# Preparation and first attention merged into one pipeline, with the bf16 remainders' subtractions on VectorE

## The reference

```python
def _L0_xattn_ref(q, k, v):          # q = layernorm(x), k = v = ctx_2048
    b, d, m = q.shape                # 64, 64, 256;  h = 8 heads
    qh = q.reshape(b * h, d // h, m)
    kh = k.reshape(b * h, d // h, -1)
    vh = v.reshape(b * h, c // h, -1)
    scale = 1.0 / jnp.sqrt(d // h)
    qk = jnp.einsum('bdm,bdn->bmn', qh, kh) * scale
    sm = jax.nn.softmax(qk, axis=-1)
    ret = jnp.einsum('bmn,bcn->bcm', sm, vh)
    return ret.reshape(b, c, m)

x = x + _L0_xattn_ref(_layernorm(x, axis=-1), ctx_2048, ctx_2048)
```

## Time and profile before

| | |
|---|---|
| Three runs | 2029.39, 2031.86, 2032.33 us |
| Median | 2031.86 us |
| Profiled execution, its span | 2031.3 us |
| TensorE (PE) busy | 1408.2 us, 69% |
| VectorE (DVE) busy | 1363.5 us, 67% |
| ScalarE (ACT) busy | 1120.5 us, 55% |
| GpSimd (POOL) busy | 497.0 us, 24% |
| First score matmul of the attention | 134.1 us |
| First instruction of the stage behind the attention | 580.1 us |

### The profile page before, as it was taken

The page is one execution under the profiler, slowest core; times in us unless marked ns, Lnnn a source line. Parts: engine busy times, 40 slices in busy tenths (PEclk is TensorE's granted clock), DMA queues, the critical chain, the costliest instruction groups (busy, mean ns, idle before and its releaser), DMA issues. The chain is left out here.

```text
span 2031.3 us, 33248 instructions
## 1 busy us (share of the span) xinstructions
PE 1408.2 (69%) x11186; PEld 870.4 (43%) x11186; DVE 1363.5 (67%) x2850; ACT 1120.5 (55%) x1552; POOL 497.0 (24%) x903
## 2 busy tenths in 40 slices
PE   4429999999929894999626667379999646674111
PEld 4305555555527771555411333246565423342100
DVE  6646888888634534588867999535555468875896
ACT  4516777777712222677637888633434237875554
POOL 4411233333320004111013343200101001112663
PEclk9999999999959996999855766689999958877555
DMA  5652555555330003233110000011010120000111
GB/s 168 204 131 54 123 131 132 131 129 131 87 86 1 0 1 59 49 73 76 33 67 0 0 1 1 16 42 43 22 41 22 34 87 1 0 1 11 42 52 42
DMA packets 96387, 117.99 MB, mean 58 GB/s; under 512 B 29728, under 2 KB 82152, under 8 KB 91660
## 3 DMA queue, kind: packets, MB, share of 16 engines
q1 hardware_dynamic: 96268, 116.46, 23.0%
HBM read 80.07 MB, written 22.88 MB: 51 GB/s over the span
## 5 line engine op out<-in xcount | busy, mean ns | idle before, releaser
L610 DVE TENSOR_REDUCE ratt_nmax<-ratt_psS 128x2 f32<-128x512 f32 x512 | 318.7, 684 | 100.3 <-PE ratt_psS L502 98.7
L576 ACT ACTIVATE ratt_E<-ratt_psT 128x1024 f32<-128x1024 f32 x256 | 255.1, 1023 | 111.7 <-PE ratt_psT L524 111.6
L502 PE MATMUL ratt_psS<-ratt_K,ratt_Q 72*128 72x256 bf16 x1024 | 205.0, 285 | 42.9 <-DMA ratt_K<-context_parts 37.7
L524 PE MATMUL ratt_psT<-ratt_Q,ratt_K 75*128 75x256 bf16 x1024 | 196.8, 276 | 7.6 <-DMA ratt_Q<-ratt_rows 7.2
L502 PEld LDWEIGHTS ratt_psS<-ratt_K,ratt_Q 72*128 72x128 bf16 x1024 | 80.3, 99 | 139.5 <-issue 67.5
L537 PE MATMUL ratt_psO<-ratt_E,ratt_V 128*32 128x256 f32 x2048 | 138.8, 389 | 0.7 <-ACT ratt_E L576 0.7
L524 PEld LDWEIGHTS ratt_psT<-ratt_Q,ratt_K 75*128 75x128 bf16 x1024 | 99.9, 99 | 25.8 <-DMA ratt_Q<-ratt_rows 7.7
L3393 PE MATMUL final_psT<-final_identh,final_Z 128*128 128x128 f16 x64 | 8.3, 311 | 110.2 <-ACT final_Z L3427 110.2
L2195 PE MATMUL nffn_psH<-nffn_W,nffn_QT 128*128 128x512 bf16 x128 | 56.2, 589 | 28.8 <-ACT nffn_H L2274 19.9
L537 PEld LDWEIGHTS ratt_psO<-ratt_E,ratt_V 128*32 128x32 f32 x2048 | 53.8, 110 | 50.9 <-issue 28.1
L892 ACT COPY sffn_XS<-sffn_psG 128x512 f32<-128x512 f32 x8 | 4.7, 586 | 124.0 <-PE sffn_psG L841 124.0
(11 more groups left out here) (472 smaller groups left out, 3703.4 us busy)
## 6 DMA issues: line engine op xcount, KB each, us to landing
ratt_Q<-z_parts SPq DMA_DIRECT2D x32, 576.0 KB
ratt_K<-context_parts SPq DMA_DIRECT2D x96, 192.0 KB
gatt_V<-in_ctx_dram SPq DMA_DIRECT2D x16, 512.0 KB, 6.3
z_parts<-prep_ZS SPq DMA_DIRECT2D x48, 128.0 KB, 2.6
context_parts<-prep_CS SPq DMA_DIRECT2D x48, 128.0 KB, 2.3
head_sums<-ratt_O SPq DMA_DIRECT2D x64, 72.0 KB
all_X<-in_x_dram SPq DMA_DIRECT2D x8, 512.0 KB
prep_C<-in_ctx_dram SPq DMA_DIRECT2D x8, 512.0 KB
```

What stands on the lines that cost most here:

```text
L502: mm = nc.tensor.matmul(psS[:, RING[h], c * D:(c + 1) * D], Q9[0:R, buf, h, k % 2, c * P:(c + 1) * P], K9[0:R, buf, h, k % 2, :], start=Tr ...
L524: mm = nc.tensor.matmul(psT[:, p % 2, e, c, :], K9[0:RM, buf, h, u, c * P:(c + 1) * P], Q9[0:RM, buf, h, u, :], start=True, stop=True)
L576: nc.scalar.activation(E[:, 2 * b + p // 2, 2 * (p % 2):2 * (p % 2) + 2], psT[:, p % 2], ACT.Exp, scale=SCALE).then_inc(exped, 1)
L610: nc.vector.tensor_reduce(nmax[:, k % 2, h, :], psS[:, RING[h]].rearrange("p (c t) -> p c t", c=2), AX.X, ALU.max, negate=True).then_inc(m ...
```

## The change

The two functions become one, `first_attention`. Its slots begin at n = -12 (LEAD), and the preparation of a pair of tiles (a, 16 of them, in place of eight groups of four tiles) is spread over the slots 4a - 12 to 4a - 4, in the same per-engine programs as the attention: `at(n, r)` gives the pair whose step r falls on slot n. There is no barrier between the two, and no loop: all slots are written out. The parts of C and Z have one buffer for a pair, Z one, C two; the remainders overwrite C and Z. By step: 0 loads, 1 transpose of C (into the ring psT) and VectorE's statistics, 2 aggregates, first part and remainder of C, 3 GpSimd's root and second part of C, 4 normalisation, third part of C, product with the weights, 5 first part of Z and the sum for ST, 6 remainder and second part of Z, 7 third part of Z. A part is stored one slot later or in the same one (steps 3 to 8).

The engines of some steps differ from before: all four subtractions are VectorE's (C's were GpSimd's), the two second parts' casts are GpSimd's (were ScalarE's), the third parts are written by the subtraction itself, in bf16 (were a subtraction and a cast of ScalarE's), the normalisation is ScalarE's (was VectorE's), and ST comes from a product of GpSimd's and a reduction of VectorE's (was TensorE's). The functions of the attention's own steps stay as they are, but for the ring psT, in which the transpose of C takes a place.

```diff
@@ -74,226 +74,7 @@
-def prepare(nc, io, X, CT, ident, zq, ck, ST, wsum):
...
-def row_attention(nc, io, X, CT, ident, identb, zq, ck, o_dram, r_dram):
+def first_attention(nc, io, X, CT, ident, identb, zq, ck, o_dram, r_dram, ST, wsum):
...
+    LEAD = 12
+    WEIGHTS = 9
...
+        C = s.sb("C", [P, 2, 2, D])
+        Z = s.sb("Z", [P, 2, D])
+        CS = s.sb("CS", [P, 3, 2, D], BF16)
+        ZS = s.sb("ZS", [P, 3, 2, D], BF16)
...
+        def at(n, r):
+
+            a, left = divmod(n + LEAD - r, 4)
+            return a if left == 0 and is_pair(a) else None
+
+        job, jobs = {}, 0
+        for n in range(-LEAD, UNITS + LAG + 1):
+            for p in range(4):
+                if is_unit(n - LAG):
+                    job["shift", n - LAG, p] = jobs
+                    jobs += 1
...
+                def load_x(a):
+                    if a > 1:
+                        sp.wait_ge(x_in[a % 2], a // 2 * 16)
+                    sp.dma_start(X[:, 2 * a:2 * a + 2, :],
+                                 x_dram[2 * a:2 * a + 2].rearrange("t p d -> p t d")).then_inc(x_in[a % 2], 16)
+
+                def load_c(a):
+                    if a > 1:
+                        sp.wait_ge(c_third, a - 1)
+                    sp.dma_start(C[:, a % 2],
+                                 c_dram[2 * a:2 * a + 2].rearrange("t p d -> p t d")).then_inc(c_in[a % 2], 16)
+
+                def store_c(a, part):
+                    sp.wait_ge((c_first, c_second, c_third)[part], a + 1)
+                    sp.dma_start(ck.rearrange("r s a h u m -> s a h r (u m)")[part, a],
+                                 CS[:, part].rearrange("p u m -> p (u m)")).then_inc(c_out, 16)
+
+                def store_z(a, part):
+                    sp.wait_ge((z_first, z_second, z_third)[part], a + 1)
+                    sp.dma_start(zq.rearrange("s r a h u m -> s a h r (u m)")[part, a],
+                                 ZS[:, part].rearrange("p u m -> p (u m)")).then_inc(z_out, 16)
+
...
+                for n in range(-LEAD, UNITS + 11):
                     if is_unit(n - 1):
+                        bring_row(n - 1)
+                    if n % 2 and is_unit(n + 3):
+                        load_q((n + 3) // 2)
+                    if n % 2 == 0 and is_unit(n + 2):
+                        load_k((n + 2) // 2)
+                    c = n // 4 - 2
+                    if n % 4 == 0:
+                        if is_pair(c - 1):
+                            inverses_out(c - 1)
+                        if is_pair(c):
+                            out(c)
+                    if n % 4 == 1 and is_pair(c):
+                        sums_back(c)
+                    if n % 4 == 2 and is_pair(c - 1):
+                        back(c - 1)
+                    if at(n, 0) is not None:
+                        load_x(at(n, 0))
+                        load_c(at(n, 0))
+                    for part in range(3):
+                        if at(n, 3 + part) is not None:
+                            store_c(at(n, 3 + part), part)
+                        if at(n, 6 + part) is not None:
+                            store_z(at(n, 6 + part), part)
...
+                def root(a):
+                    pool.wait_ge(z_agg, a * 2 + 2)
+                    gp.tensor_tensor(veps[:], mv[:, :, 1], eps[:], ALU.add).then_inc(z_pool, 1)
+                    pool.wait_ge(z_pool, a * 3 + 1)
+                    if a > 0:
+                        pool.wait_ge(z_done, a * 2)
+                    gp.tensor_tensor(rstd[:], veps[:], mhalf[:], ALU.pow).then_inc(z_pool, 1)
+                    pool.wait_ge(z_pool, a * 3 + 2)
+                    gp.tensor_tensor(shift[:, 0], mv[:, :, 0], rstd[:], ALU.mult).then_inc(z_pool, 1)
+                    pool.wait_ge(z_pool, a * 3 + 3)
+                    gp.tensor_tensor(shift[:, 1], none[:], shift[:, 0], ALU.subtract).then_inc(z_shift, 1)
+
+                def second_of_z(a):
+                    pool.wait_ge(z_rest, a + 1)
+                    gp.tensor_copy(ZS[:, 1], Z[:]).then_inc(z_second, 1)
+
+                def second_of_c(a):
+                    pool.wait_ge(c_rest, a + 1)
+                    gp.tensor_copy(CS[:, 1], C[:, a % 2]).then_inc(c_second, 1)
+
+                def weigh(a):
+                    pool.wait_ge(exped, job["turn", a] + 1)
+                    if a == 0:
+                        pool.wait_ge(w_steps, WEIGHTS)
+                    if a > 0:
+                        pool.wait_ge(st_done, a)
+                    gp.tensor_tensor(product[:].rearrange("p k b l -> p (k b) l"),
+                                     CT[:, :, a * 4 * L:(a + 1) * 4 * L].rearrange("p k (b l) -> p k b l", l=L),
+                                     spread(spread(wrow[:], 1, 4), 1, KC), ALU.mult).then_inc(weighed, 1)
+
...
+                    if at(n, 3) is not None:
+                        root(at(n, 3))
+                        second_of_c(at(n, 3))
+                    if at(n, 4) is not None:
+                        weigh(at(n, 4))
+                    if at(n, 6) is not None:
+                        second_of_z(at(n, 6))
...
+                def turn_context(a):
+                    j = job["turn", a]
+                    pe.wait_ge(c_in[a % 2], a // 2 * 16 + 16)
+                    if j > 1:
+                        pe.wait_ge(exped, j - 1)
+                    for k in range(KC):
+                        for t in range(2):
+                            mm = nc.tensor.transpose(psT[:, j % 2, 0, k, t * P:(t + 1) * P],
+                                                     C[:, a % 2, t, k * P:(k + 1) * P], ident[:])
+                    mm.then_inc(written, 1)
...
+                        if p == 1 and at(n, 1) is not None:
+                            turn_context(at(n, 1))
...
+                def take_context(a):
+                    j = job["turn", a]
+                    act.wait_ge(written, j + 1)
+                    sc.copy(CT[:, :, a * 2 * P:(a + 1) * 2 * P], psT[:, j % 2, 0]).then_inc(exped, 1)
...
+                def normalise(a):
+                    act.wait_ge(z_shift, a + 1)
+                    if a > 0:
+                        act.wait_ge(z_third, a)
+                    for t in range(2):
+                        sc.activation(Z[:, t], X[:, 2 * a + t, :], ACT.Identity, bias=shift[:, 1, t:t + 1],
+                                      scale=rstd[:, t:t + 1]).then_inc(z_done, 1)
+
+                def first_of_z(a):
+                    act.wait_ge(z_done, a * 2 + 2)
+                    if a > 0:
+                        act.wait_ge(z_out, a * 48)
+                    sc.copy(ZS[:, 0], Z[:]).then_inc(z_first, 1)
+
+                def first_of_c(a):
+                    act.wait_ge(c_in[a % 2], a // 2 * 16 + 16)
+                    if a > 0:
+                        act.wait_ge(c_out, a * 48)
+                    sc.copy(CS[:, 0], C[:, a % 2]).then_inc(c_first, 1)
...
+                    if at(n, 2) is not None:
+                        first_of_c(at(n, 2))
+                    if at(n, 4) is not None:
+                        normalise(at(n, 4))
+                    if at(n, 5) is not None:
+                        first_of_z(at(n, 5))
...
+                def rest_of_z(a):
+                    dve.wait_ge(z_first, a + 1)
+                    v.tensor_tensor(Z[:], Z[:], ZS[:, 0], ALU.subtract).then_inc(z_rest, 1)
+
+                def third_of_z(a):
+                    dve.wait_ge(z_second, a + 1)
+                    v.tensor_tensor(ZS[:, 2], Z[:], ZS[:, 1], ALU.subtract).then_inc(z_third, 1)
+
+                def rest_of_c(a):
+                    dve.wait_ge(c_first, a + 1)
+                    dve.wait_ge(written, job["turn", a] + 1)
+                    v.tensor_tensor(C[:, a % 2], C[:, a % 2], CS[:, 0], ALU.subtract).then_inc(c_rest, 1)
+
+                def third_of_c(a):
+                    dve.wait_ge(c_second, a + 1)
+                    v.tensor_tensor(CS[:, 2], C[:, a % 2], CS[:, 1], ALU.subtract).then_inc(c_third, 1)
+
+                def sum_context(a):
+                    dve.wait_ge(weighed, a + 1)
+                    v.tensor_reduce(ST[:, :, 4 * a:4 * a + 4], product[:], AX.X, ALU.add).then_inc(st_done, 1)
...
+                    if at(n, 1) is not None:
+                        take_stats(at(n, 1))
+                    if at(n, 2) is not None:
+                        aggregate(at(n, 2))
+                    if at(n, 2) is not None:
+                        rest_of_c(at(n, 2))
+                    if at(n, 4) is not None:
+                        third_of_c(at(n, 4))
+                    if at(n, 5) is not None:
+                        sum_context(at(n, 5))
+                    if at(n, 6) is not None:
+                        rest_of_z(at(n, 6))
+                    if at(n, 7) is not None:
+                        third_of_z(at(n, 7))
...
-        prepare(nc, io, X, CT, ident, zq, ck, ST, wsum)
-        row_attention(nc, io, X, CT, ident, identb, zq, ck, o_dram, r_dram)
```

(5 more changed lines are left out.)

600 lines of the change are left out of this document (224 added, 376 removed).

## The result

The changed kernel takes 2090.0 us (median of four runs), the kernel before 2030.6 us on the same chip: a ratio of 1.029, 95% interval 1.027 to 1.031. It is slower, by 59.4 us. The forecast was 2072 us in a range of 1985 to 2118. The profiled execution has a span of 2086.7 us against 2031.3.

The account below looks back on a forecast made before the run. TensorE was taken to bound the attention, with no engine full in the preparation before it. 2031.3 - 107 (earlier start) = 1924, + 20 (added work) + 94 (waits for C's load) + 34 (lower clock) = 2072 us; range 1985 to 2118.

Parts of the forecast that it names:

- slot 3: First attention slot with shifted scores: at about 49 us, in place of 156.7 in the kernel before.
- waits for C behind the first scores: TensorE before C's transpose, pairs 4 to 15: load issued too late, 12 waits of 7.8 us, 94 us.
- clock: TensorE at the lower clock for 5.2 us after each C wait: 2.8 us lost, 12 times, 34 us.
- all the rest, above 1924: Preparation's added work in the attention's slots: 1.5 us a pair over 13 pairs, 20 us on top of 1924.
- rival 3: C's load lands in time, preparation hides, VectorE limits: 1961 us, faster; 0.26 with what lies between it and rival 2.
- The preparation beside the attention: Preparation's work merged into the attention's slots: 1.0 us a pair on VectorE, 0.5 on TensorE; 20 us over 13 pairs.
- VectorE's wait: Slot with residue 2: VectorE waits for ScalarE's cast of C, costing 1.0 us a pair, bounds 0 and 2.5.
- The subtractions: Four over 512 elements a pair on VectorE: 0.7 us each taken, 0.61 free, 1.2 if blocked by GpSimd.
- 1: Rival: each of 12 C stalls is followed by 15 us at the slow clock, adding 48 us: 2120; chance 0.13.
- 2: Rival: C stall at its lower bounds, 85 us with clock: 2022 to 2035, not slower; 0.13 with what lies near.
- 4: Rival: GpSimd late with the maxima's split, 16 us if 1 us in each of 16 pairs; only shifts the others.
- 5: Rival: only C's two subtractions change engine, worth under 1 us a pair alone; the rest is merging; no chance given.

Follow-up runs that it names:

- h1: g6 plus 60 matmuls with overwritten results on TensorE in front of the wait for C (pairs a > 3): 2050.0 us, ratio 1.009.
- g6: Changed kernel with its late load kept, plus a semaphore for each of the three stored parts of C and Z: 2089.6 us, ratio 1.029.
- g3: Changed kernel with X and C loaded one slot earlier (slot 4a - 13) and a semaphore for each stored part: 1958.7 us, ratio 0.965.
- g4: g3 with ScalarE's cast of C moved from the end to the middle of its slot: 1956.3 us, ratio 0.964.
- h3: g3 with the subtractions of C alone on GpSimd, those of Z on VectorE: 1962.9 us, ratio 0.967.
- h4: Changed kernel (late load, one semaphore for three parts) with the subtractions of C alone on GpSimd: 2082.7 us, ratio 1.027.
- h2: Changed kernel with X and C loaded in the same slot but ahead of its Q, K, inverses and O, plus a semaphore for each part: 1990.9 us, ratio 0.980.

## Why the prediction was right

**The direction and the mechanism** hold, step by step:

| step | forecast | measured |
|---|---|---|
| first score matmul | 33 us | 33.57 |
| slot 3 | 49 us | 51.85 |
| waits for C behind the first scores | 12 of 7.8 us, 94 us | 12 of 7.2 us, 86.2 us |
| their distance | 34 to 40 us | 36.6 to 37.4 us eight times, 41.9 to 42.2 three times |
| clock | 34 us | 39.6 us (h1 under g6), some 50 by the rows |
| wait and clock together | 128 us | 130.9 us (g6 against g3) |
| all the rest, above 1924 | 20 us | 35 us (g3) |
| time with no wait (rival 3) | 1961 us | 1958.7 (g3) |
| next stage | near 620 us | 634.75 |
| VectorE's busy share | 0.7 | 0.63 |

**The wait.** C was issued 3.2 us after TensorE wanted it (forecast 2.75) and was there 4.2 us later (forecast 5.1). Both were built from rows of another program, and the errors partly cancel: 7.4 in this cycle for 7.8. The order of issues in SyncE's slot was what the earlier trace rows let one expect; X's issue alone took 1.90 us where 0.42 had been taken. Its landing was 3.8 us in the median of these slots, between the two ends of the earlier trace rows.

**The clock.** The low rate lasts 7.0 us in the cycle shown and 6.4 to 8.1 in the nine regular pairs, nearer to the 5.2 us of the earlier trace rows than to the 15 us of the earlier trace rows. A regular pair takes 37.0 us (the mean of the eight distances) against 4 x 6.72 = 26.9 in g3 (238 maxima in 200 us, 8 to a slot). Of the 10.1 us between them 7.2 are the wait: 2.9 are left, where 2.8 had been taken. What the forecast did not have are the other three pairs, which take 42 us: their slow rows behind the wait last 11.8 us, and then the rate falls a second time, for 5.5 to 5.9 us. Over all twelve pairs the slow rows add up to 119 us, 9.9 a pair, where the sum had 5.2. In the pair from 224.79 the matmuls are back at 0.38 us only from 236.6 on; then comes the 1.13 us wait for VectorE that ends at 242.55, and from 244.71 to 250.2 they are slow once more. The windows of that stretch:

```profile
core 0: us, PE busy (x) PEld busy (x) DVE busy (x) ACT busy (x) POOL busy (x), PEclk, DMA share, GB/s
224.70:232.00 7.30, 7.21 (x41) 4.34 (x42) 4.08 (x8) 3.29 (x5) 1.26 (x5) 0.50 0.05 15
232.00:245.00 13.00, 11.80 (x97) 6.22 (x95) 9.03 (x16) 7.55 (x10) 2.65 (x9) 0.76 0.47 115
245.00:259.00 14.00, 13.93 (x130) 8.31 (x128) 11.44 (x19) 9.77 (x14) 7.19 (x18) 0.81 0.45 119
```

Three such cycles of 5 us more are 15 us. With 12 x 2.9 the clock would so cost 50 us by the rows, where the filler won 40 (g6 to h1); h1 is not at the full clock throughout either, 0.95 to 1.00 in its four windows of 100 us from 100 to 500. The true share lies near these two, above the 34 us of the forecast.

**The preparation beside the attention** is the term that was mis-sized, with the clock's second fall. The sum said 1924 + 20 us with the wait left out; g3 stands 35 us above 1924. Its next stage starts at 501.14, 79.0 us earlier than before, where 107 had gone from the front: 28 us are within the stage, and 26.9 - 25.1 = 1.8 us a pair over up to 16 pairs gives 29, for the 1.5 us over 13 that were taken. From there to the end g3's span has 4.0 us more than the kernel before, and the cause of these is open. Its median lies 2.4 above its span (1956.3); 1.7 of this stand between time and span of one and the same execution (1958.03 and 1956.3), which the sum had put at nothing. What the 1.8 us a pair are made of was not tested: TensorE's rows in g3 have four transposes a pair and waits for VectorE (1.12 us) and for K. Against the forecast of 2072, the 18 us more are so: wait 8 less, this term 15 more, and the clock 6 more by h1 or some 15 by the rows, which gives 13 or 22. That the total is so near is in part luck: the wait was put too high and the two other terms too low. VectorE's wait was right in place and size: 1.0 us in each pair was forecast in the slot with the residue 2, and TensorE waits for VectorE 18 times for 16.9 us, with these rows of VectorE and TensorE at one of these waits:

```profile
359.09 0.69 DVE L562 TENSOR_TENSOR ratt_C<-ratt_C,ratt_CS 128x512 f32<-128x512 f32 x1 [0.92 <-ACT ratt_CS L511]
359.70 0.69 DVE L553 TENSOR_TENSOR ratt_Z<-ratt_Z,ratt_ZS 128x512 f32<-128x512 f32 x1
```

```profile
361.05 0.39 PE L387 MATMUL ratt_psS<-ratt_K,ratt_Q 72*128 72x256 bf16 x2 [1.13 <-DVE ratt_nmax L574]
```

But g4, which takes the wait away, is not faster by what it lasted: K's load is the next to be late.

**The subtractions** take 0.69 us on VectorE (forecast 0.7) and 1.15 on GpSimd. This is the view of the tile CS (line, operation, count: ns least, median, most):

```profile
L562 DVE TENSOR_TENSOR ratt_C<-ratt_C,ratt_CS x16: 691/693/694, 9.0 to 512.4; 128x512 f32<-128x512 f32 x16
...
L566 DVE TENSOR_TENSOR ratt_CS<-ratt_C,ratt_CS x16: 681/682/1736, 10.4 to 525.0; 128x512 bf16<-128x512 f32 x16
```

VectorE is hardly ever held: L562 never, L566 twice in its 16, in the start, where GpSimd's product (L324, 1.26 us) began 0.07 us before it. In the attention it is the other way round: there the subtraction begins first, and GpSimd's instruction is the one that lasts longer. The rows of one of the two, of a later subtraction, and of the same GpSimd instruction with no subtraction beside it:

```profile
10.34 1.26 POOL L324 TENSOR_TENSOR ratt_product<-all_CT,ratt_factors 128x512 f32<-128x512 f32 x1
10.41 1.74 DVE L566 TENSOR_TENSOR ratt_CS<-ratt_C,ratt_CS 128x512 bf16<-128x512 f32 x1 [0.57 <-POOL ratt_CS L316]
...
371.61 0.68 DVE L566 TENSOR_TENSOR ratt_CS<-ratt_C,ratt_CS 128x512 bf16<-128x512 f32 x1
371.77 0.64 POOL L344 TENSOR_TENSOR ratt_parts<-ratt_nmax,ratt_zero 128x16 bf16<-128x16 f32 x1 [2.47 <-DVE ratt_nmax L574]
...
387.50 0.27 POOL L344 TENSOR_TENSOR ratt_parts<-ratt_nmax,ratt_zero 128x16 bf16<-128x16 f32 x1 [11.02 <-DVE ratt_nmax L574]
```

Every third part of C and Z that VectorE writes from the first scores on has the first or the second instruction of the maxima's split beside it, 28 times, and each of these takes 0.64 to 0.66 us in place of 0.27 or 0.23. The Trainium skill (SBUF — State Buffer, Who interferes with whom) says that a two-input VectorE instruction and a GpSimd instruction reading SBUF exclude each other. The trace agrees, in both directions. No run here moves the one instruction away from the other alone. The 1.0 to 2.5 us a pair that the prediction worked out from the rule did not come, because in the attention VectorE was first each time: what is blocked is GpSimd, by some 0.4 us a subtraction, and GpSimd has room (101 us busy in 300).

**Rivals.** 1 falls as it stands: no return of the clock took 15 us, but with 9.9 us slow in the mean of the twelve pairs it was about halfway there. 2 falls (86 us of waiting, not 67). 3 did not happen. Its number (1961) was nearly that of the kernel in which its condition was met (g3, 1958.7), but in part by luck: it had put 37 us down to VectorE, and in g3 TensorE waits 16.6 us for VectorE and 20.5 for K. 4: TensorE's waits show none for GpSimd's split. 5 holds: the name's part could not be told from nothing (h3, h4), the rest is the merging.

## What to carry to other kernels

When a preparation is merged into a loop, look at each new load for the slot in which its user stands, and issue it at least one slot before: here one slot was worth 80 us of 2090 by itself and 131 with the stores' semaphores, and the engine of the subtractions some 8, hardly clear of the noise. A wait on the critical path hides the ones beneath it (52 us of the stores' here), so after taking it away the profile has to be read afresh. One semaphore that counts several parts of a single buffer makes the first writer wait for the last reader; one for each part costs no memory, and with the early load it gave the fastest kernels here, 1956.3 us (g4) and 1958.7 (g3), which beat the kernel before by 3.5% and the changed one by 6%.

## What the runs showed of the hardware

A stall of TensorE cost more than its length here, 1.3 to 1.7 us for each us by the four figures under h2, as TensorE came back at the lower clock; the filler, which took that away, won 40 us of 131. And short gaps did not all do the same. The 1.12 or 1.13 us wait for VectorE comes once a pair in the changed kernel. In three pairs TensorE had worked slowly for 11.8 us behind C's wait and fast for some 4.8 us when the gap began, and the clock fell again, for 5.5 to 5.9 us; in the nine others, with 6.4 to 8.1 us slow and 6.8 to 7.7 us fast ahead of it, it did not. In g3, at the higher level from 58 us on but for one stretch, the same gap comes in every pair and did not lower the rate by itself; a wait of 1.65 us for K at 139.7 us, 6.6 us behind one of them, did, until 150.5, and a wait of 1.92 us for K at 441.3 did not. In h2 four waits for C of 2.09 to 2.67 us all did, of eight of 1.10 to 1.64 us one did, and behind four of its 1.12 us waits for VectorE the rows were slow for 1.2 to 1.7 us. What decides between them stays open. The row of g3's wait at 139.7:

```profile
139.70 0.39 PE L396 MATMUL ratt_psS<-ratt_K,ratt_Q 72*128 72x256 bf16 x2 [1.65 <-DMA ratt_K<-context_parts]
```

Matmuls without a use, issued in the wait, held the clock in most pairs and won 40 us. Subtractions of 512 elements take 682 or 693 ns on VectorE (bf16 or f32 written) and 1152 on GpSimd; moving two of them changed the time by no more than could be told from nothing. A subtraction on VectorE and a GpSimd instruction of 128x16 that began 0.05 to 0.17 us behind it: 0.64 us for GpSimd's in place of 0.27; with GpSimd's first by 0.07 us, 1.74 us for VectorE's in place of 0.68.
